# Folded weights stored without duplicate rows, later head loads on SyncE's queue, each pair stored behind its rope columns

## The reference

```python
xn = layernorm(x)
kv_c = xn @ W_kvd + b_kvd                     # 64 wide
q_c  = xn @ W_qd + b_qd                       # 192 wide
k = concat(heads(kv_c @ W_ku + b_ku, 128), rope(heads(kv_c @ W_kr + b_kr, 64)))
q = concat(heads(q_c @ W_qu + b_qu, 128),  rope(heads(q_c @ W_qr + b_qr, 64)))
v = heads(kv_c @ W_vu + b_vu, 128)
probs = softmax(causal(q @ k.T / sqrt(192)))
out = x + (probs @ v) @ W_o + b_o + xn @ binarized(W_ffn).T + b_ffn
```

## Time and profile before

| | us |
|---|---|
| median of 3 runs | 1452.0 |
| lowest, highest | 1451.02, 1452.54 |
| span of the profiled execution | 1452.4 |
| TensorE busy in it | 1405.6 |
| ScalarE busy | 1203.6 |
| VectorE busy | 1155.3 |
| GpSimd busy | 992.0 |

### The profile page before, as it was taken

The page is one execution under the profiler, slowest core; times in us unless marked ns, Lnnn a source line. Parts: engine busy times, 40 slices in busy tenths (PEclk is TensorE's granted clock), DMA queues, the critical chain, the costliest instruction groups (busy, mean ns, idle before and its releaser), DMA issues.

```text
span 1452.4 us, 27576 instructions
## 1 busy us (share of the span) xinstructions
PE 1405.6 (97%) x9826; PEld 1278.5 (88%) x9826; DVE 1155.3 (80%) x2756; ACT 1203.6 (83%) x2553; POOL 992.0 (68%) x571
## 2 busy tenths in 40 slices
PE   6789999999999999999999999999999999999997
PEld 4679999998899999998898999998889999999987
DVE  5568898876778888887677888888677888888887
ACT  4458889997788888898687888899777988888886
POOL 5667767867667667768665777777765776666750
PEclk9899999999999999999999999999999999999998
DMA  7952322121323322211233222221232322221100
GB/s 221 304 165 58 92 63 60 51 63 49 87 66 102 91 63 63 63 33 46 77 91 81 61 86 63 63 59 52 62 74 75 94 62 63 63 63 48 37 23 30
DMA packets 39997, 111.27 MB, mean 77 GB/s; under 512 B 7685, under 2 KB 16182, under 8 KB 39862
## 3 DMA queue, kind: packets, MB, share of 16 engines
q1 hardware_dynamic: 35152, 92.69, 23.6%
q0 software_dynamic: 4544, 16.78, 3.4%
q10 hardware_dynamic: 166, 0.03, 0.0%
HBM read 49.71 MB, written 13.63 MB: 44 GB/s over the span
## 4 chain that ended last, share of the span: by engine, by line
PE 83%; ACT 6%; POOL 3%; DVE 3%; DMA 3%; issue 1%; SPq 1%; POOLq 0%; DVEq 0%; ACTq 0%
PE turn L1472 16%; PE ring L1417 11%; PE u_ps L1490 8%; PE ring L1449 8%; PE ring L1447 8%; PE u_ps L1491 8%; PE ring L1448 8%; PE o_ps L1510 4%; PE o_ps L1511 4%; PE ring L1430 2%; ACT probs L737 2%; PE ring L1362 1%; PE ring L1356 1%; POOL k_rope L321 1%; DVE probs L1006 1%; DMA wv_scratch<-wv_parts 1%
## 5 line engine op out<-in xcount | busy, mean ns | idle before, releaser
L1006 DVE TENSOR_SCALAR_CACHE_REDUCE probs<-ring,c_t 128x1024 f32<-128x1024 f32 (+7 forms) x512 | 413.6, 809 | 106.1 <-PE ring L1449 101.2
L1016 DVE TENSOR_TENSOR probs_lo<-turn,probs_hi 128x512 fp32r<-128x512 f32 (+1 forms) x640 | 401.0, 630 | 69.2 <-ACT probs_hi L746 64.4
L746 ACT ACTIVATE probs_hi<-turn 128x512 fp32r<-128x512 f32 (+1 forms) x640 | 350.7, 550 | 115.0 <-PE turn L1472 109.0
L737 ACT ACTIVATE probs<-probs,row_min 128x1024 f32<-128x1024 f32 (+7 forms) x512 | 394.3, 771 | 11.7 <-DVE probs L1006 9.1
L1472 PE MATMUL turn<-ident,probs 128*128 128x128 f32 x2304 | 386.6, 275 | 6.0 <-ACT probs L737 3.7
L1490 PE MATMUL u_ps<-probs_hi,kv_nat 128*128 128x256 f32 x1152 | 315.2, 303 | 0.0
L1472 PEld LDWEIGHTS turn<-ident,probs 128*128 128x128 f32 x2304 | 286.5, 141 | 31.8 <-ACT probs L737 9.3
L1491 PE MATMUL u_ps<-probs_lo,kv_nat 128*128 128x256 f32 x1152 | 290.7, 282 | 0.0
L1447 PE MATMUL ring<-k_hi,q_hi 128*128 128x512 f32 (+2 forms) x768 | 280.0, 365 | 0.0
L1449 PE MATMUL ring<-k_hi,q_lo 128*128 128x512 f32 (+2 forms) x768 | 263.9, 344 | 0.0
L1448 PE MATMUL ring<-k_lo,q_hi 128*128 128x512 f32 (+2 forms) x768 | 263.1, 343 | 0.0
(11 more groups left out here) (229 smaller groups left out, 2590.6 us busy)
## 6 DMA issues: line engine op xcount, KB each, us to landing
wp<-wp_scratch SPq DMA_DIRECT2D x31, 640.0 KB, 4.1
swapped<-k_rope SPq DMA_DIRECT2D x128, 128.0 KB, 2.3
wv<-wv_scratch SPq DMA_DIRECT2D x31, 512.0 KB, 3.3
swapped<-q_y SPq DMA_DIRECT2D x62, 128.0 KB, 2.3
swapped<-q_x SPq DMA_DIRECT2D x62, 128.0 KB, 2.3
wp_scratch<-wp_parts POOLq DMA_DIRECT2D x7, 640.0 KB, 5.6
k_hi<-qb_kv_hi SPq DMA_DIRECT2D x16, 256.0 KB, 3.7
k_lo<-qb_kv_lo SPq DMA_DIRECT2D x16, 256.0 KB, 5.0
```

The source lines that it names most:

```text
L737: act.activation(p, p, ACT.Exp, scale=-1.0, bias=row_min[:, r:r + 1], accum_out=row_sum[:, g % 4, w, h:h + 1]).then_inc(exp_ready, 1)
L746: act.activation(probs_hi[:, r % 4, 0:width], turn[r % 2][:, 0:width], ACT.Identity).then_inc(turned_hi, 1)
L1006: dve.tensor_scalar(probs_of(g, w, h), ring[slot_of(entry)][:, KEY_COLUMN[qt]:KEY_COLUMN[qt] + keys], c_t[b % 2][:, qt, ds(pair * 2 + h, 1 ...
L1016: dve.tensor_tensor(probs_lo[:, r % 4, 0:width], turn[r % 2][:, 0:width], probs_hi[:, r % 4, 0:width].bitcast(F32), ALU.subtract).then_inc ...
```

## The change

Stores: of `wp`, the first chunk's columns go out with 128 rows, the second chunk's and the key columns with 64 rows only; of the values, 64 rows of high and 64 of low part. The columns of `wp` are put in another order so that each of these is one block, and those of `wv` so that the part comes ahead of the head. Four transfers per pair take the place of two. Loads rebuild the doubled rows: `load_wp` takes three transfers (one of 128 rows, and the 64-row block twice), `load_wv` two (the high part once more beside itself by a stride of zero, and high and low). ScalarE's copy of the high part into rows 0 to 63 is left out for pairs 1 to 7, since it isn't stored. Head loads 2 and 3 go from GpSimd's queue to SyncE's: load 2 ahead of `stack(0)`, load 3 behind it. On GpSimd each pair is stored right behind its rope columns.

```diff
+def query_column(part, h, rows):
+    return rows * WA + (part * 2 + h) * P
+def key_column(part):
+    return 2 * WA + part * WK
...
-    wp_dram = nc.dram_tensor("wp_scratch", (PAIRS, P, WP_COLS), F32R).ap()
-    wv_dram = nc.dram_tensor("wv_scratch", (PAIRS, P, WV_COLS), F32R).ap()
+    wp_dram = nc.dram_tensor("wp_scratch", (PAIRS, P * WA + 64 * (WP_COLS - WA)), F32R).ap()
+    wv_dram = nc.dram_tensor("wv_scratch", (PAIRS, 64 * WV_COLS), F32R).ap()
+    def wp_rows(p, all_rows):
+        flat = wp_dram[ds(p, 1)]
+        if all_rows:
+            return flat[:, 0:P * WA].rearrange("a (p c) -> (a p) c", p=P).bitcast(F32)
+        return flat[:, P * WA:].rearrange("a (p c) -> (a p) c", p=64).bitcast(F32)
+    def wv_rows(p):
+        return wv_dram[ds(p, 1)].rearrange("a (p q c) -> (a p) q c", p=64, q=2).bitcast(F32)
+    def value_rows(values, rows):
+        return values[rows, :, :, :].rearrange("p q h n -> p q (h n)").bitcast(F32)
... load_wp
-                sp.dma_start(wp[:, :].bitcast(F32), wp_dram[ds(m % PAIRS, 1)].rearrange("a p c -> p (a c)").bitcast(F32)).then_inc(wp_loaded, 16)
+                sp.dma_start(wp[:, 0:WA].bitcast(F32), wp_rows(m % PAIRS, True)).then_inc(wp_loaded, 16)
+                for rows in (slice(0, 64), slice(64, P)):
+                    sp.dma_start(wp[rows, WA:WP_COLS].bitcast(F32), wp_rows(m % PAIRS, False)).then_inc(wp_loaded, 16)
... load_wv
-                sp.dma_start(wv[m % 2][:, :, :, :].rearrange("p a b c -> p (a b c)").bitcast(F32),
-                             wv_dram[ds(m % PAIRS, 1)].rearrange("a p c -> p (a c)").bitcast(F32)).then_inc(wv_loaded, 16)
+                highs = wv_rows(m % PAIRS)[:, 0:1, :].to_broadcast([64, 2, 2 * HID])
+                sp.dma_start(value_rows(wv[m % 2], slice(0, 64)), highs).then_inc(wv_loaded, 16)
+                sp.dma_start(value_rows(wv[m % 2], slice(64, P)), wv_rows(m % PAIRS)).then_inc(wv_loaded, 16)
... SyncE
+            def load_heads_again(turn):
+                sp.wait_ge(head_turned, (turn - 1) * LOAD_HEADS)
+                heads = slice(turn * LOAD_HEADS * HD, (turn + 1) * LOAD_HEADS * HD)
+                sp.dma_start(qu_a[turn % 2][:, :], W_qu[0:P, heads]).then_inc(turn_loaded[turn], 16)
+                for to, source in ((qu_b, W_qu[P:QC, heads]), (vu, W_vu[:, heads]), (ku, W_ku[:, heads])):
+                    for rows in (slice(0, 64), slice(64, P)):
+                        sp.dma_start(to[turn % 2][rows, :], source).then_inc(turn_loaded[turn], 16)
...
             load_heads(1)
+            load_heads_again(2)
             stack(0)
+            load_heads_again(3)
             swap(0, 0)
... GpSimd: load_heads taken out, and
-                pool.dma_start(wp_dram[p].bitcast(F32), parts[:, :].bitcast(F32)).then_inc(stored_p, 16)
-                pool.dma_start(wv_dram[p].bitcast(F32), values[:, :, :, :].rearrange("p a b c -> p (a b c)").bitcast(F32)).then_inc(stored_p, 16)
+                pool.dma_start(wp_rows(p, True), parts[:, 0:WA].bitcast(F32)).then_inc(stored_p, 16)
+                pool.dma_start(wp_rows(p, False), parts[0:64, WA:WP_COLS].bitcast(F32)).then_inc(stored_p, 16)
+                for part, rows in enumerate((slice(0, 64), slice(64, P))):
+                    pool.dma_start(wv_rows(p)[:, part, :], value_rows(values, rows)[:, part, :]).then_inc(stored_p, 16)
...
-            rope_columns(0)
-            rope_columns(1)
-            load_heads(2)
-            rope_columns(2)
-            store_parts(0)
-            store_parts(1)
-            load_heads(3)
-            store_parts(2)
-            for p in range(3, PAIRS):
+            for p in range(PAIRS):
                 rope_columns(p)
                 store_parts(p)
             residual(0)
... ScalarE, folded_high
-                act.activation(values[:, h, 0, :], f[:, 256:512], ACT.Identity)
-                act.activation(values[0:64, h, 1, :], f[0:64, 256:512], ACT.Identity).then_inc(fold_hi, 1)
+                last = act.activation(values[:, 0, h, :], f[:, 256:512], ACT.Identity)
+                if p == 0:
+                    last = act.activation(values[0:64, 1, h, :], f[0:64, 256:512], ACT.Identity)
+                last.then_inc(fold_hi, 1)
```

More of the change, by code:

```diff
@@ L96, in is_block @@
     return 0 <= g < STEPS * BLOCKS
-WQ = 2 * 2 * P
+WA = 2 * 2 * P
 WK = P
-WP_COLS = 2 * WQ + 2 * WK
+WP_COLS = 2 * WA + 2 * WK
 WV_COLS = 2 * 2 * HID
+WP_LOADS, WV_LOADS, PARTS_STORES = 3, 2, 4
 B_QU, B_KU, B_VU, B_KR, B_QR, B_DOWN = 0, NH, 2 * NH, 3 * NH, 3 * NH + PAIRS, 3 * NH + 2 * PAIRS
@@ L109 @@
 NORM_STEPS = 10
+def query_column(part, h, rows):
+    return rows * WA + (part * 2 + h) * P
+def key_column(part):
+    return 2 * WA + part * WK
 def wq_part(parts, part):
-    return parts[:, part * WQ:(part + 1) * WQ].rearrange("p (a b c) -> p a b c", a=2, b=2)
+    return parts[:, 0:2 * WA].rearrange("p (b q h c) -> p q h b c", b=2, q=2, h=2)[:, part]
 def wk_part(parts, part):
-    return parts[:, 2 * WQ + part * WK:][:, 0:WK]
+    return parts[:, key_column(part):][:, 0:WK]
 def build(nc, x, W_kvd, b_kvd, W_ku, b_ku, W_vu, b_vu, W_kr, b_kr, W_qd, b_qd, W_qu, b_qu, W_qr, b_qr,
           W_o, b_o, W_ffn, b_ffn, cos_t, sin_t, out):
-    wp_dram = nc.dram_tensor("wp_scratch", (PAIRS, P, WP_COLS), F32R).ap()
-    wv_dram = nc.dram_tensor("wv_scratch", (PAIRS, P, WV_COLS), F32R).ap()
+    wp_dram = nc.dram_tensor("wp_scratch", (PAIRS, P * WA + 64 * (WP_COLS - WA)), F32R).ap()
[9 more added lines that the diff above has]
+        return values[rows, :, :, :].rearrange("p q h n -> p q (h n)").bitcast(F32)
     with ExitStack() as ctx:
@@ L256, in wait_stored @@
         def wait_stored(engine, p):
-            engine.wait_ge(parts_stored[0 if p == 0 else 1 + (p - 1) % 2], 32 * (1 if p == 0 else (p - 1) // 2 + 1))
+            engine.wait_ge(parts_stored[0 if p == 0 else 1 + (p - 1) % 2], 16 * PARTS_STORES * (1 if p == 0 else (p - 1) // 2 + 1))
         def slot_of(entry):
@@ L551, in rope_columns @@
                     pool.wait_ge(rope_w_ready, done + part + 1)
[L553 to L560, removed]
             def load_wo(c):
@@ L1210, in folded_low @@
                                          in1=wq_part(parts, 0)[:, h, :, to].bitcast(F32), op0=ALU.mult, op1=ALU.subtract)
-                dve.tensor_tensor(values[64:P, h, 1, :], f[64:P, 256:512], values[64:P, h, 0, :].bitcast(F32), ALU.subtract)
+                dve.tensor_tensor(values[64:P, 1, h, :], f[64:P, 256:512], values[64:P, 0, h, :].bitcast(F32), ALU.subtract)
                 dve.tensor_scalar(bias_p[to, p:p + 1, QUERY_X + h], f[to, 130:131], -SCALE, None, ALU.mult)
@@ L1404, in project_pair @@
                     else:
-                        pe.wait_ge(wp_loaded, m * 16)
+                        pe.wait_ge(wp_loaded, m * (16 * WP_LOADS))
                 for c in range(2):
@@ L1408, in project_pair @@
                     if k == ROPE_K:
-                        hi, lo = (wp[:, 2 * WQ + part * WK:][:, 0:P] for part in range(2))
+                        hi, lo = (wp[:, key_column(part):][:, 0:P] for part in range(2))
                         passes = ((hi, kv_stack), (lo, kv_stack))
@@ L1413, in project_pair @@
                         (a_hi, b_hi), (a_lo, b_lo) = (
-                            [wp[:, part * WQ + (h * 2 + rows) * P:][:, 0:P] for rows in range(2)] for part in range(2))
+                            [wp[:, query_column(part, h, rows):][:, 0:P] for rows in range(2)] for part in range(2))
                         passes = ((a_hi, qa_hi), (a_hi, qa_lo), (a_lo, qa_hi), (b_hi, qb_stack), (b_lo, qb_stack))
@@ L1501, in output @@
                 if n == 0 and w == 0 and m > 0:
-                    pe.wait_ge(wv_loaded, m * 16)
+                    pe.wait_ge(wv_loaded, m * (16 * WV_LOADS))
                 pe.wait_ge(u_ready, count + 1)
@@ L1509, in output @@
                     head = slice(h * P, (h + 1) * P)
-                    pe.matmul(o_ps[:, h, :], u_hi[w][:, head], wv[slot][:, h, 0, :], start=True, stop=False)
-                    mm = pe.matmul(o_ps[:, h, :], u_pair[w][:, head], wv[slot][:, h, 1, :], start=False, stop=True)
+                    pe.matmul(o_ps[:, h, :], u_hi[w][:, head], wv[slot][:, 0, h, :], start=True, stop=False)
+                    mm = pe.matmul(o_ps[:, h, :], u_pair[w][:, head], wv[slot][:, 1, h, :], start=False, stop=True)
                 mm.then_inc(o_full, 1)
```

## The result

Beside the kernel before on one chip, the changed kernel took 1443.48 us (4 executions, 1442.03 to 1444.93) against 1452.27 (4): ratio 0.9939, 95% interval 0.9925 to 0.9954. Over all 16 executions the median is 1446.0. So it is faster, by 8.8 us of the medians in the first comparison and 4.4 in the second; forecast were 7.5. The profiled execution is the fastest of the 16, 1442.03 with a span of 1440.2, and its rows have to be read beside those of e9.

A forecast was written before the change was run, and what follows sets the result against it. TensorE bounds the 32 steps, unchanged, so the gain lies in the head, with its DMA waits: 5.4 + 2.0 = 7.4 us; 1452.4 - 7.4 - 0.4 = 1444.6, said as 1444.5, range 1440 to 1451.

The forecast's parts named there:

- Load 2 collides, rope weights 3.5 us late: Head, 16 to 30 us: load 2 on SyncE adds 3.5 us of DMA work, delaying GpSimd's rope weights; bounds 0 and 4.2.
- no collision: Rival, chance 0.2: load 2 slips into the idle 30 to 36, all gates come 3.5 sooner: -10.9, 1441.
- the two landings of another stretch: SyncE's swap issued at 57.13 was in by 64.42; GpSimd's store issued at 50.56 only at about 64.0.
- First gate, -4.2: ScalarE's first wait in the head, for the store of pair 1, ends at 49.7 instead of 53.95: -4.2 us.
- X's swap last, VectorE in time for it, -5.4: Head: VectorE, ready in time, starts X's rope after SyncE's swap at 59.0 instead of 64.42: -5.4 us.
- Clock, -2.0 of 0 to 2.6: Head, fold of head 8 to natural projections: TensorE's drop to 0.50 clock not expected, 2.0 us gained of 0 to 2.6.
- Costed at nothing: GpSimd's work up to its residual, and the steps' five loads for two with shorter wp rows, were to add no time.
- the cover of 3.3 us: GpSimd needs until 85.6 for stores and residual; the swap it waits for comes at 88.9: covered by 3.3.
- the third rival: GpSimd becomes the bound: at 6.3 us a pair it needs 92.0, 3.1 beyond the swap: -4.3, 1448; chance 0.07.
- The steps the same within a microsecond: Sign: from step 1's first projection to the end, the length stays as before, within a microsecond.

The follow-up runs named there:

- e9: The changed kernel run again unchanged, 12 executions: 1446.47 us, ratio 0.9966 against the kernel before.
- e6: The changed kernel with head load 2 held on SyncE until the rope weights are in: 1443.84 us, ratio 0.9947.
- e7: The changed kernel with GpSimd's old order, three pairs of rope columns ahead of the first stores: 1447.51 us, ratio 0.9968.
- e2: The kernel before with only the short rows stored and the rebuilding loads: 1448.15 us, ratio 0.9975.
- e5: The changed kernel with head load 3 behind the rope keys' swap on SyncE: 1447.61 us, ratio 0.9976.
- e8: The changed kernel with head load 3 issued by GpSimd behind the store of pair 2: 1447.55 us, ratio 0.9966.
- e1: The changed kernel with full 128-row stores and loads as before, new order and SyncE loads kept: 1452.47 us, ratio 1.0000.
- e4: The kernel before with only head loads 2 and 3 moved to SyncE: 1449.42 us, ratio 0.9982.
- e11: The changed kernel with two first_linear tiles moved ahead of fold(10) on TensorE: 1444.76 us, ratio 0.9950.
- e12: e7 with two first_linear tiles moved ahead of fold(10) on TensorE: 1445.63 us, ratio 0.9963.
- e10: The changed kernel with one first_linear tile moved ahead of fold(10) on TensorE: 1444.82 us, ratio 0.9953.
- e13: e6 and e11 together, load 2 held and two tiles moved: 1442.80 us, ratio 0.9951.

## Why the prediction was right, and which steps were not

The time was right: 1443.5 and 1446.5 in the two comparisons, for 1444.5. The place, the head, was right in part: up to step 1's first projection it gives 8.8 us in the first profile and 3.5 in e9's, for 7.4, and the steps behind give 3.3 and 2.1 that the sum had at nothing. Of its terms:

- **Load 2 collides, rope weights 3.5 us late.** Wrong for the rope weights, and there the rival "no collision" had it: they are in at 23.52, and e6 showed that holding load 2 back changes nothing for them. The collision itself is there, but it meets what GpSimd issues beside load 2: `cos` lands 14.9 us after its issue for 9.8 before, a delay not far from the size of the term. So the queues are served together, as the two landings of another stretch had let me argue; the step that failed is which transfers are hit. The rope weights had been issued by 15.3, load 2 came from 17.63 on, and no engine waits for `cos`. The Trainium skill's rule ("DMA: Bandwidth & Descriptors", Queues, rings and completion order) has each DMA engine going round the queues with work. The landings of `cos` agree with it. The stretch of 30 to 36 is full (0.09 to 1.04 of the DMA engines) with load 2 and, from 32.95 on, the store of pair 0. That rival's price, 10.9 us, didn't come, for the reason in the third point.
- **First gate, -4.2.** It is -7.0 (53.95 to 46.95). The store of pair 1 is issued by 41.0 instead of 45.4, since the rope weights aren't late; it lands 5.95 us later, not 4.3. But the gate is off the path: e7 opens it 3.9 us later at no cost that shows, and e2 has it at 53.76 and gains.
- **X's swap last, VectorE in time for it, -5.4.** The sum is near (64.42 to 58.07, -6.4; in e9 60.14, -4.3), the mechanism isn't. X begins at 51.78, for 51.1, but behind 1.95 us of waiting for TensorE's projection and not behind the gate. VectorE stands for the rope keys' swap, which I had left out: I let load 3 be issued from 41 to 45, and it took SyncE from 39.33 to 47.26, 8 us for 7 transfers. From the swap's landing at 53.12, VectorE's own work of 4.95 us leads to X without a pause. e5 and e8 show that load 3's place on SyncE isn't what lies behind it: issued from 45.89 and 45.86 on, the swap is in at 52.94 and 54.95. The amount of data posted between 38 and 58 is left, argued and not shown. The stored bytes may count here too: e1 differs from the changed kernel in the rows alone (and ScalarE's copies for them), and in e1 SyncE gets to that swap 3.8 us later than in the first profile, 2.2 later than in e9's. That the loads alone gain 2.5 us (e4) and nothing with the new order and full rows (e1) fits with it, but one profile of each is little, where two of the same program differ by 1.6 us in that issue (47.31 and 48.86).
- **Clock, -2.0 of 0 to 2.6.** -2.4 in the first profile (19.6 to 17.2), +0.9 in e9 (20.5). I took it as a property of the kernel; it differs between executions of one program, together with the pause ahead of `fold(10)` (0.84 and 3.54 us). With tiles moved into that pause the clock is 1.00 in 62 to 68 in all four profiles, and natural comes 17.2 us behind in three. That the pause alone decides isn't shown (e11 and e12 above).
- **Costed at nothing.** GpSimd's residual ends at 87.23 and the rope follows at 87.34 without idle time: the cover of 3.3 us is used up in the first profile, which was to be the sign of the third rival, at no cost that shows: natural to step 2 took 43.2 us for 43.4 before. In e9 GpSimd waits 1.51 us for that swap. Five loads for two in the steps cost nothing that shows: among TensorE's waits none is for a load of `wp` or `wv`. The Trainium skill's advice against transfers to disjoint partition halves ("DMA: Bandwidth & Descriptors", Rules for kernel authors) does not speak for the cut, and e2, which has these loads, was faster and not slower. What the cut costs by itself no run shows.
- **The steps the same within a microsecond.** Wrong by 1.7 to 4.0 us, to the good. From step 2's first projection to the end, the three profiled kernels with full rows (before, e1, e4) took 1323.7 to 1323.9 us, the eleven profiles with short rows 1319.7 to 1322.0. The change's two profiles: 1320.4 and 1321.6, for 1323.7. This weighs: e1's head ends where e9's does (step 1's first projection at 85.40 and 85.47), so between these two profiles the steps make all of the difference. Nor are the steps equal, as I had it: before, steps 2 to 30 take 39.8 to 55.3 us from one first projection to the next. Most of the gain lies at two changes of batch, where TensorE's clock fell to 0.50 before and mostly not after. From step 16's first projection to step 17's it takes 45.9 us in the three profiles with full rows and 44.3 to 44.4 in the eleven others; from step 24's to step 25's 45.9 in the three and also in e9 and e11, 44.3 to 44.4 in the other nine. At the first change of batch, from step 8's to step 9's, it is 44.3 to 44.4 in all fourteen. The pause ahead and the window behind it at step 16, before first, then the changed kernel:

```profile
766.62 0.23 PE L1430 MATMUL ring<-mask_bf,ident_bf 128*128 128x128 bf16 x1 [0.94 <-DVE probs L1006]
```

```profile
770.00:772.00 2.00, 2.00 (x11) 2.00 (x10) 1.80 (x4) 1.12 (x4) 1.88 (x1) 0.50 0.00 0
```

```profile
757.58 0.23 PE L1458 MATMUL ring<-mask_bf,ident_bf 128*128 128x128 bf16 x1 [0.93 <-DVE probs L1034]
```

```profile
761.00:763.00 2.00, 2.00 (x18) 1.91 (x17) 1.51 (x4) 1.80 (x5) 1.88 (x1) 1.00 0.00 0
```

In both TensorE is busy all of the 2 us, DMA moves nothing, and the pause ahead is alike (0.94 and 0.93 us for VectorE's softmax). Two profiles with short rows (e9, e11) have the fall at step 24 all the same, so the format of the rows doesn't decide it alone. Why it should matter there was not found; it stays open.

So a right number came partly from errors that cancelled: a delay that the rope weights didn't have (+3.5 on the gate) stood in for the rope keys' swap, which is late and was left out, and the steps gave 2.1 to 3.3 us that the sum didn't have. That 7.5 lies between the two measured gains, 4.4 and 8.8, is partly luck.

## What to carry to other kernels

Where the DMA engines are full, look for the transfer that is wanted next and count what is posted beside it on all queues; what was issued well ahead wasn't touched here (the rope weights), what was issued beside the new load was (`cos`). Moving one load past another changed who waits (e5, e8). Fewer bytes gained by themselves (e2), but not at the two waits that they were to shorten: find the gain by stages over the whole span, the ones put at nothing too. And where TensorE pauses for another engine, independent products in the pause may keep the clock up behind it (e10, e11); here that gain is told from zero only against one of the changed kernel's two series.

## What the runs showed of the hardware that was not expected

- The same program spread over 1442.4 to 1451.2 us in twelve executions, and its two profiles differ by 6.8 us: four executions were too few for a difference of 5 us. The first four lie 3.5 us under these twelve in the mean.
- 1.05 MB more on SyncE's queue, issued from 17.63 on, left GpSimd's loads issued by 15.3 where they were (in at 23.52 for 25.03) and took the one issued at 18.73 from 9.8 to 14.9 us.
- SyncE's issue of one transfer took about 0.6 us at 18 to 22 (`ku`, 1.24 for two) and 1.5 us at 40 to 43 (`qu_b`, 2.97 for two), with the DMA engines full both times (1.04 and 0.94). Load 3 took SyncE 8 us in the changed kernel and 10.5 in e1. What makes the difference wasn't tried.
- The length of one pause doesn't tell TensorE's clock behind it: in e11 it stayed at 1.00 in 58 to 62 behind a pause of 2.66 us, in e13 it was 0.63 there behind one of 2.35; and behind 0.94 us at the change from batch 1 to 2 it fell to 0.50 in the kernel before.
